# Loading x on SyncE's queue, storing its bf16 copy on ScalarE's, and quantizing the hidden rows one tile later, in a post-norm transformer layer

## The reference, cut to what matters

```
x = layernorm(x + attn(x))          # qkv and proj: 8 groups, 128 inputs each
x = layernorm(x + ffn(x))

def attn(x):
    q, k, v = grouped_linear(x, w_qkv)              # w_qkv: (8, 128, 384)
    a = softmax(q * 64**-0.5 @ k.T)
    return grouped_linear(a @ v, w_proj) + b_proj   # w_proj: (8, 128, 128)

def ffn(x):                                         # inner width 4096
    h = silu(bitlinear(x, w_gate)) * bitlinear(x, w_up)
    return bitlinear(h, w_down)

def bitlinear(x, w):     # act_quant: 127 / max|row|, round; weight_quant: 1 / mean|w|, round to -1, 0, 1
    return act_quant(x) @ weight_quant(w).T
```

## Time and profile before

| what | value |
|---|---|
| time, median of 2 runs | 2144.16 us (2143.17 to 2145.16) |
| the profiled execution | 2152.84 us |
| its span on the slowest core (core 2) | 2150.6 us |
| spans of the eight cores | 2127.8 to 2150.6 us |
| TensorE matmul busy | 1345.2 us (63%) |
| ScalarE busy | 939.3 us (44%) |
| VectorE busy | 924.7 us (43%) |
| DMA, mean over the span | 146 GB/s |
| first stage, up to the first Q/K eviction | 0 to 159.5 us |
| gate/up, block oc = 7 of half 0 and of half 1 | about 1385 to 1485 us and 1677 to 1772 us |

### The profile page before, as it was taken

One profiled execution on the slowest core, in us unless ns is written; L12 is line 12 of the kernel. 1 busy time (PEld: TensorE's weight loads), 2 busy tenths in 40 slices (PEclk: granted clock), 3 DMA queues, 4 the chain that ended last, 5 costly groups with the idle time before them and its releaser, 6 DMA issues.

```text
span 2150.6 us, 20542 instructions; the slowest of 8 cores (2127.8 to 2150.6 us)
## 1 busy us (share of the span) xinstructions
PE 1345.2 (63%) x5439; PEld 467.2 (22%) x5502; DVE 924.7 (43%) x1742; ACT 939.3 (44%) x1079; POOL 44.6 (2%) x84
## 2 busy tenths in 40 slices
PE   0007776477747773067663899856999647776682
PEld 0002111111111110011111344412444212222231
DVE  1015872463567334584518444444444440303023
ACT  1119888488838884058870121254121550101011
POOL 0000000000000000000000000000000000000000
PEclk9999888688868886578875899968999769888796
DMA  4468992135752788836804433333444326667572
GB/s 155 134 189 268 321 318 80 34 81 142 192 160 80 204 217 219 229 89 179 236 11 115 101 77 76 75 111 98 92 96 94 112 102 167 172 171 185 157 217 82
DMA packets 371458, 314.02 MB, mean 146 GB/s; under 512 B 296593, under 2 KB 298641, under 8 KB 369298
## 3 DMA queue, kind: packets, MB, share of 16 engines
q1 hardware_dynamic: 339712, 230.78, 41.8%
q10 hardware_dynamic: 23186, 52.58, 7.1%
q0 software_dynamic: 8448, 29.37, 3.6%
HBM read 161.49 MB, written 83.89 MB: 114 GB/s over the span
## 4 chain that ended last, share of the span: by engine, by line
PE 42%; ACT 14%; DMA 14%; DVE 12%; SPq 8%; issue 7%; ACTq 2%; DVEq 0%; POOLq 0%
PE ps L84 42%; ACT A L84 14%; SPq L84 8%; DVE A L84 8%; DMA wdt_sb<-wdqT_s 3%; DMA A<-wg 2%; DVE ln_sb L84 2%; DMA xt_s<-A 2%; ACTq L84 2%; DMA wtstage<-wdq_s 2%; DMA A<-wqkv 1%; DMA A<-wproj 1%; DVE h L84 1%; DMA wdqT_s<-wtstage 1%; DMA A<-wu 1%
## 5 line engine op out<-in xcount | busy, mean ns | idle before, releaser
L84 PE MATMUL ps<-A,A 64*128 64x512 bf16 (+1 forms) x2048 | 533.6, 435 | 204.1 <-ACT A L84 179.8
L84 ACT ACTIVATE A<-ps,cst_sb 128x1024 bf16<-128x1024 f32 (+1 forms) x544 | 551.9, 1117 | 243.6 <-DVE A L84 157.0
L84 PE MATMUL ps<-wg_sl,xqT 128*128 128x512 bf16 x1003 | 265.5, 409 | 113.5 <-DVE h L84 98.6
L84 PE MATMUL ps<-wdt_sb,hqT 128*128 128x512 bf16 x1003 | 252.6, 411 | 111.5 <-DMA wdt_sb<-wdqT_s 54.8
L84 PEld LDWEIGHTS ps<-A,A 64*128 64x128 bf16 (+1 forms) x2048 | 126.0, 106 | 609.8 <-issue 606.4
L84 ACT ACTIVATE A<-ps,scg 128x512 f32<-128x512 f32 x128 | 87.9, 687 | 331.9 <-PE ps L84 309.6
L84 DVE SCALAR_TENSOR_TENSOR h<-ps,scu,A 128x512 bf16<-128x512 f32 x128 | 96.1, 751 | 217.8 <-ACT A L84 213.6
L84 DVE TENSOR_SCALAR A<-A 128x1024 f32<-128x1024 f32 (+1 forms) x208 | 144.4, 694 | 39.4 <-DVE A L84 17.3
L84 PEld LDWEIGHTS ps<-wdt_sb,hqT 128*128 128x128 bf16 x1024 | 103.8, 104 | 260.2 <-issue 162.6
L84 DVE TENSOR_SCALAR A<-A,wsc 128x1024 f32<-128x1024 f32 x96 | 72.3, 753 | 201.8 <-DMA A<-wg 96.7
L84 PEld LDWEIGHTS ps<-wg_sl,xqT 128*128 128x128 bf16 x1024 | 104.2, 103 | 251.0 <-issue 145.3
(11 more groups left out here) (66 smaller groups left out, 699.2 us busy)
## 6 DMA issues: line engine op xcount, KB each, us to landing
A<-wg SPq DMA_DIRECT2D x64, 512.0 KB, 5.9
A<-wu SPq DMA_DIRECT2D x64, 512.0 KB, 5.8
A<-wd SPq DMA_DIRECT2D x64, 512.0 KB, 6.1
wdt_sb<-wdqT_s SPq DMA_DIRECT2D x128, 256.0 KB, 3.5
hq_s<-h ACTq DMA_DIRECT2D x16, 1024.0 KB, 3.9
A<-x ACTq DMA_DIRECT2D x16, 512.0 KB, 3.5
xt_s<-A POOLq DMA_DIRECT2D x16, 512.0 KB, 3.0
A<-xt_s ACTq DMA_DIRECT2D x16, 512.0 KB, 3.7
```

The source lines that it names most:

```text
L84: ins = getattr(eng, meth)(*args, **kw)
```

## The change

Two places change.

In the first stage the x loads move to SyncE's list and the xbf_s stores to ScalarE's. The load of tile i is now emitted in step i (its wait for the slot's xt_s store is on SyncE), and the store of the bf16 copy comes directly behind the cast, with a wait of ScalarE for its own cast. The transposes stay on SyncE.

In the block oc = 7, `emit_quant_store` for tile t - 1 comes behind Silu, product and maximum of tile t; that of the last tile follows at once on that of the one before. Silu gets a further wait in this block, on VectorE's counter c_v, all but its last increment.

```diff
-    def emit_xload(i):
-        p4 = i % 4
-        if i >= 4:
-            wait("scalar", f"s_xts{p4}", 16 * (i // 4))
-        dma("scalar", xslot(i), x_d[i * 128:(i + 1) * 128, :], f"s_x{p4}")
-
-    for i in range(min(4, T)):
-        emit_xload(i)
     for i in range(T):
...
-        nn = 16 * (i // 4 + 1)
+        if i >= 4:
+            wait("sync", f"s_xts{p4}", 16 * (i // 4))
+        nn = dma("sync", xst, x_d[i * 128:(i + 1) * 128, :], f"s_x{p4}")
...
-        wait("sync", "c_xc", i + 1)
-        dma("sync", xbf_s[i * 128:(i + 1) * 128, :], xbst, f"s_xbf{par}")
+        wait("scalar", "c_xc", i + 1)
+        dma("scalar", xbf_s[i * 128:(i + 1) * 128, :], xbst, f"s_xbf{par}")
...
-        if i + 4 < T:
-            emit_xload(i + 4)
...
+                if oc == 7:
+                    wait("scalar", "c_v", max(0, c("c_v") - 1))
...
                 if oc == 7:
-                    emit_quant_store(s, t)
+                    if t >= 1:
+                        emit_quant_store(s, t - 1)
+                    if t == ST - 1:
+                        emit_quant_store(s, t)
```

## The result

| | before | after |
|---|---|---|
| time, median | 2152.04 us (10 runs) | 2099.37 us (11 runs) |
| ratio, 95% interval | | 0.9764 [0.9731, 0.9797] |
| the profiled execution | 2152.84 us | 2099.16 us |
| span of the slowest core | 2150.6 us | 2096.9 us |

The change makes the kernel faster by 2.4% (95% interval 2.0% to 2.7%): 50.8 us by the ratio, for 56.5 forecast. By the same ratio the 2144.16 us that were shown with the kernel before become 2093.6, and the forecast was 2087.7.

A forecast was written before the change was run, and what follows sets the result against it. It took queue-order waits to bound the first stage and serial ScalarE and VectorE work to bound oc 7; -48.3 + 0.2 - 8.4 = -56.5 us gave 2087.7 us from the shown median of 2144.16, range 2078 to 2109.

The forecast's parts named there:

- The front is bound by waits in ScalarE's list, not by its work: First stage: nothing is saturated; ScalarE's x load for a later tile waits for an xt_s store, holding up its queue.
- the first step: First stage, cast of tile 0 to cast of tile 1: 7.49 us would become 1.55, 5.9 us gained.
- part A: First stage, x loads on SyncE and xbf stores on ScalarE: first Q/K eviction at 111.2 us for 159.47, -48.3 us.
- the eight tiles with weight loads: 4.73 us each: First stage, tiles 1 to 8: cast to first weight load 1.55 us for 6.28, 37.8 us gained in all.
- the first rival: First stage: the DMA engines take back a part of the gain, -35 us in all, 2109 us; chance 14%.
- The stretch from cast 9 to the first eviction: End of the first stage: x loads pace casts 9 to 11, at 80.5, 82.9 and 85.4 us; evictions start at 111.2.
- The start: First stage, cast 0: x requested at once, so cast at 9.45 us instead of 10.67, 1.2 us gained.
- x late behind a set: First stage: x loads queue behind eight transposes; tile 5's is hidden, tile 9 loses 2 us, tile 13's x comes at 104.8.
- Nothing later holds the gain back: Attention and all later stages move with the first stage; VectorE's weight means have 63.6 us of slack.
- Part B: Block oc 7, deferred quantization: no overlap, period stays 11.87 us; +0.2 us in the first half, -8.4 in the second.
- the down stage as long as before: Sign that the forecast is right: the down projection, though starting earlier, takes no longer than before.
- Nothing later looks at that one: Second half, end of oc 7: nothing needs the last quantization for tens of microseconds, so down starts 8.4 us earlier.

The follow-up runs named there:

- stores_only: The kernel before with only the xbf_s stores moved to ScalarE's list, the x loads left there too; ratio to before 0.9990.
- trains_at_end: The changed kernel with all four sets of transposes behind the last x load on SyncE's list; ratio to before 0.9714.
- bias_first: The changed kernel, but SyncE waits for the bias row before the first x load; one profiled execution, no ratio, first Q/K eviction at 119.5 us for 119.8.
- quant_only: The kernel before with only the block oc = 7 (deferred quantization) as changed; ratio to before 0.9960.
- quant_pipelined: The changed kernel with separate Silu buffers, four piece buffers, the previous tile's scale ahead of the product, GpSimd issuing the hq_s store, no ScalarE self-wait; ratio to before 0.9489.
- pipelined_scalar_store: quant_pipelined with the hq_s store back on ScalarE's list, between the pieces of tile t-1 and the Silu of tile t+1; ratio to before 0.9469.

## Why the prediction was right, and where its sizes were off

- **The front is bound by waits in ScalarE's list, not by its work: right.** The wait for xt_s is gone, the first step went from 7.4 to 1.6 us (forecast 7.49 to 1.55) and steps 2-3 and 3-4 from 12.9 to 7.7 and 8.9 (forecast 8.1). stores_only shows that it was the loads' place.
- **The size of part A: 48.3 us forecast, 41.0 measured.** The term that was mis-sized is "the eight tiles with weight loads: 4.73 us each", 37.8 us in all; they gave 28.7. The two steps beside transposes gave 0.4 and 1.5 us of their 9.5 (16.1 to 15.7, 14.7 to 13.1), the other six 3.3 to 5.3 us each, 26.8 of their 28.4. I had taken the weight loads beside transposes to stay as slow as they were in the earlier trace rows, but in the changed kernel more meets the transposes: x loads on their heels, the engines full (1.02), and a weight load of 8.77 us. trains_at_end confirms that transposes and held-back x loads are the cause: without them both steps are as short as their neighbours. This is the first rival, "the DMA engines take back a part of A", in a mild form: it was priced at 21 us and took 7.5. The other losses are 0.8 us at the start and 1.6 in the six steps, nearly all of it in step 1-2 (9.8 us, and 10.1 in trains_at_end), for which no experiment gives a cause.
- **Luck in part A.** The stretch from cast 9 to the first eviction gave 6.2 us (36.2 to 30.0) where the forecast had 3.3. The forecast paced casts 9 to 11 by the x loads; in fact ScalarE came so much later to tile 9 that x was mostly there, and these steps took 1.6, 2.9 and 2.0 us. This gain of 2.9 us hides a part of the loss above.
- **The start: too large, by little.** 1.2 us of gain were forecast for cast 0, 0.4 came. The first bias copy came 1.7 us later than before, since the bias row shares the engines with four x loads (3.8 us for 2.1 on the mean of the cores, 4.55 for 1.48 on the slowest core of each). bias_first shows that this decides nothing.
- **x late behind a set: right at tile 13, half right at tile 9.** All eight cores wait for tile 13's x, 16.5 to 17.7 us, with a step of 18.2 us. At tile 9, where 2 us were forecast on the core used for it, four of eight wait 1.1 to 4.1 us and four not at all (core 1, shown above, doesn't), and one core waits 1.2 us at tile 5. By the rule of the Trainium skill ("DMA: Bandwidth & Descriptors", Queues, rings and completion order), x on SyncE's queue starts behind its transposes; tile 13's load took 4.11 us in the chain, between the 4.8 used by the rule and the 3.5 without it, so the trace does not decide it. What held x back was SyncE's list, where the issue itself stood behind 11 us of transposes. The other rule (the same page, Issuing engines are not separate DMA queues) was weighed against the change and would have given 5 us. It is right that all queues share the engines, as the 8.8 us of a load on ScalarE's queue show, and it says nothing about what stands in front of an issue, which was the gain.
- **Nothing later holds the gain back: right.** -41.0, -41.2, -41.1, -41.5 at four places.
- **Part B is no pipelining, and gives one gap: right.** Silu distances of 3.45 and 11.87 us as forecast (the latter six times in a half, not seven: the seventh period of the sum has no Silu at its end), +0.2 forecast and -0.4 measured at the hq_s store of half 0, down earlier by 8.4 us (-49.9 + 41.5). What I left out is that the last two quantizations and their stores now run inside down, and the sign "the down stage as long as before" failed: 378.4 us for 377.0, and 381.4 in quant_only. "Nothing later looks at that one" may be true of its values and not of its transfers; that these are to blame is argued above and not shown.
- **The sum:** -41.5 at the end of half 0, -8.4 at the start of down and +1.4 in it make the 48.5 us of the spans; the ratio says 50.8, with an interval of 44 to 58 us, in which the forecast of 56.5 lies too.

## What to carry to other kernels

A load that waits for its buffer holds up all that stands behind it in the list of an engine that computes (5.2 us a tile here): put it where only loads stand, and look at what else that list holds, since a block of transposes there holds back the loads behind it and then releases them at once, on engines that are already full. When two engines hand pieces back and forth, moving one call a tile later brings no overlap if the buffers and the order of both lists still tie each tile to the last; print both lists and look for the wait between two periods, then split buffers, put the next scale first and drop the waits that no longer guard anything (11.87 to 7.16 us here). Price a moved transfer by what will fly beside it then, not by its duration now.

## What the runs showed of the hardware

- The eight activations of a tile are 0.81 us long each in the kernel before and the changed one, and 0.80 in quant_pipelined. But with a wait of ScalarE for its own last one and for VectorE in between they start every 0.90 us (7.16 us for eight), and without such waits every 0.71 us (5.75 us for eight): an activation starts before the one before it is shown as ended.
- Eight transposes of 128 KB hold SyncE for 10.3 to 11.2 us in the changed kernel (cores 0 to 2), and 32 in a row for 45 us in trains_at_end. In the stretches behind two sets, with four x loads of 512 KB each, the DMA share was 1.02, with 253 and 296 GB/s, and a 192 KB load took 8.8 us for 3.5.
- A store of 1 MB issued by GpSimd instead of ScalarE made little difference to the period beyond ScalarE's issue time of 0.34 us: 7.16 and 7.50 us a tile (quant_pipelined and pipelined_scalar_store).
